# Between two blocked factorisations: T turned and B = T u^T in place of A and A u

## The reference

```
q, k, v = projections of layernorm(x)                 # 128 features each
s_t = k . q;   u = k / (|k| + eps)
Au = A u;   denom = 1 + u . Au
A  = A - Au Au^T / denom                              # A starts as the identity
M  = M + v (s_t Au / denom)^T;   o = M q
```

## Time and profile before

| what | value |
|---|---|
| median of 3 runs | 1076.78 us (1076.72 to 1078.22) |
| profiled execution, its own time | 1076.09 us |
| its span, first to last instruction | 1074.4 us |
| PE busy | 927.1 us (86%), 11675 matmul instructions and as many weight loads |
| DVE busy | 787.6 us (73%) |
| ACT busy | 543.4 us (51%) |
| mean granted TensorE clock | 0.928 of full speed |

### The profile page before, as it was taken

How to read it: one execution, slowest core, us unless ns; L and a number is a source line. 1 busy time by engine, 2 the same in 40 slices (tenths; PEclk the granted TensorE clock), 3 DMA queues, 4 the chain that set the end, 5 groups by cost and what they waited for, 6 DMA issues and landing times.

```text
span 1074.4 us, 28516 instructions
## 1 busy us (share of the span) xinstructions
PE 927.1 (86%) x11675; PEld 715.0 (67%) x11675; DVE 787.6 (73%) x2503; ACT 543.4 (51%) x1096; POOL 301.3 (28%) x256
## 2 busy tenths in 40 slices
PE   3799999999998778587996828665899999999998
PEld 1467777777785657476894627464677777777766
DVE  6878787878679998896579779793666666665663
ACT  4678787878745344222244312100366565565574
POOL 4354444444311000000000000002756446446340
PEclk9999999999999798689999868786999999999999
DMA  5343548465437462145351000266425324334131
GB/s 153 75 106 111 139 127 202 133 135 132 119 127 223 134 164 52 30 130 129 109 159 49 5 3 4 76 153 172 100 78 109 99 70 111 97 83 115 40 79 59
DMA packets 179334, 112.47 MB, mean 105 GB/s; under 512 B 79616, under 2 KB 172160, under 8 KB 178560
## 3 DMA queue, kind: packets, MB, share of 16 engines
q1 hardware_dynamic: 162304, 93.81, 34.7%
q10 hardware_dynamic: 16896, 16.78, 5.1%
HBM read 49.16 MB, written 37.75 MB: 81 GB/s over the span
## 4 chain that ended last, share of the span: by engine, by line
PE 33%; DVE 15%; issue 1%; DMA 1%; POOL 1%; ACT 1%; SPq 0%; DVEq 0%; ACTq 0%; POOLq 0%
PE ldl_work L2044 10%; PE ldl_work L2032 10%; DVE lane_rows L1156 6%; DVE ldl_rank_one L1153 4%; PE ldl_work L2016 2%; PE ldl_work L1611 2%; DVE ldl_lane_dinv L1138 2%; PE ldl_work L1621 1%; PE ldl_work L1999 1%; PE ldl_work L2007 1%; PE ldl_work L2000 1%; PE ldl_work L1986 1%; DVE lane_rows L1134 1%; DVE lane_rows L1132 1%; PE ldl_work L1428 1%
## 5 line engine op out<-in xcount | busy, mean ns | idle before, releaser
L1797 POOL TENSOR_TENSOR T<-T,out_bv_rows 128x512 f32<-128x512 f32 x16 | 20.4, 1273 | 410.4 <-DMA out_bv_rows<-in_bqkv 404.2
L446 DVE TENSOR_TENSOR ffn_h_rest<-ffn_ps_h,ffn_h_high 128x512 f16<-128x512 f32 x128 | 86.2, 685 | 56.1 <-ACT ffn_ps_h L619 55.6
L618 ACT ACTIVATE ffn_h_high<-ffn_ps_h,b_columns 128x512 f16<-128x512 f32 x128 | 87.9, 687 | 64.6 <-PE ffn_ps_h L697 64.1
L2044 PE MATMUL ldl_work<-w_ternary,ldl_panels 128*128 128x256 f16 x512 | 118.2, 273 | 0.0
L711 PE MATMUL ffn_ps_y<-w_ternary,ffn_h_high 128*128 128x256 f16 x512 | 117.8, 273 | 0.0
L711 PE MATMUL ffn_ps_y<-w_ternary,ffn_h_rest 128*128 128x256 f16 x512 | 117.8, 272 | 0.0
L697 PE MATMUL ffn_ps_h<-ffn_xT_high,w_ternary 128*128 128x512 f16 x256 | 98.7, 386 | 11.8 <-DVE ffn_h_rest L446 11.8
L697 PE MATMUL ffn_ps_h<-ffn_xT_rest,w_ternary 128*128 128x512 f16 x256 | 98.3, 384 | 0.0
L2032 PE MATMUL ldl_work<-out_xT_high,w_ternary 128*128 128x512 f16 x256 | 97.0, 379 | 0.0
L2032 PE MATMUL ldl_work<-out_xT_rest,w_ternary 128*128 128x512 f16 x256 | 97.0, 379 | 0.0
L1945 ACT ACTIVATE ldl_work<-ldl_work,b_columns 128x512 f32<-128x512 f32 x128 | 84.2, 658 | 0.0
(11 more groups left out here) (215 smaller groups left out, 2296.4 us busy)
## 6 DMA issues: line engine op xcount, KB each, us to landing
ffn_x<-in_x SPq DMA_DIRECT2D x16, 512.0 KB, 4.7
x_scratch<-ffn_x_out ACTq DMA_DIRECT2D x16, 512.0 KB, 3.3
aT_scratch<-ffn_aT SPq DMA_DIRECT2D x16, 512.0 KB, 5.2
inv_aT<-aT_scratch SPq DMA_DIRECT2D x16, 512.0 KB, 5.1
ldl_panels<-uT_scratch SPq DMA_DIRECT2D x32, 256.0 KB, 3.1
T<-x_scratch SPq DMA_DIRECT2D x16, 512.0 KB, 3.8
uT_scratch<-ffn_uT SPq DMA_DIRECT2D x16, 256.0 KB, 5.3
inv_uT<-uT_scratch SPq DMA_DIRECT2D x16, 256.0 KB, 4.2
```

Of the source, the lines that this page charges most:

```text
L446: nc.vector.tensor_tensor(hl[n % 2][:, f], ps_h[f % 3][:], hh[n % 2][:, f], ALU.subtract).then_inc(hl_done, 1)
L618: nc.scalar.activation(hh[n % 2][:, f], ps_h[f % 3][:], ACT.Gelu, bias=c.b1[:, f:f + 1])
L2044: ins = nc.tensor.matmul(ps_y[t % 2], part[k % 2][:, f, t * P:(t + 1) * P], c.w2[:, f], start=(f == 0 and part is hh), stop=(f == FC - 1 a ...
```

## The change

The stage between the factorisations no longer makes A and A u^T. With B = T u^T, the Gram matrix is B^T D^-1 B, and the right side of the second factorisation is (D^-1 B)^T T. So:

- First phase: PE turns T (transposes with the identity as moving operand), ACT copies it into `m.W`, PE multiplies it with the first 32 columns of u^T only, DVE copies these columns of B into `m.KK` and writes them times D^-1 into `first_over_d` (a view of `ZR`). The first diagonal blocks come from these two.
- Second phase: PE makes the other 96 columns of B, ACT copies them into `m.KK`; then ACT multiplies the 96 columns of each pair with D^-1 into `m.W`, 64 instructions, in front of its first `empty`.
- In the second factorisation `inject` is replaced by `multiply`: 64 matmuls per block, one for each pair, with 128 x 32 weights (columns of D^-1 B) and a moving operand of B (panel, diagonal) or T (panel right). `diagonal(r)` waits until all of D^-1 B is there.
- T must now live until panel right 3, so the finished right sides 0 to 2 get a buffer of their own, `done_right`; `keep_d(0)` waits until ACT has read the old diagonal. Six buffers of the output stage move into `done_right`.

```
@@ factorise
+        done_right = sb("done_right", [P, NW - 1, NQ, P])
+        YR = [done_right[:, k] for k in range(NW - 1)] + [m.T[:, NQ * (NW - 1):]]
...
+            if not first and r == 0:
+                sp.wait_ge(e.products.over_d, NP)
...
+        def multiply(work, r, right, dst, alone):
+            i, seen = None, set()
+            for p, q in tile_order():
+                n = NQ * q + p
+                left = e.products.first_over_d[:, n] if r == 0 else m.W[:, n, block_of(r)]
+                start = (p // 4, q) not in seen
+                seen.add((p // 4, q))
+                i = nc.tensor.matmul(work[rows_of(q), p, dst], left, right(n), start=start, stop=alone,
+                                     skip_group_check=True)
+            return i
...
-                i = inject(work, r, m.W, every, every, r == 0)
+                i = multiply(work, r, lambda n: m.T[:, n], every, r == 0)
...
-                    i = inject(work, r, m.KK, after(r), after(r), r == 0)
+                    if first:
+                        i = inject(work, r, m.KK, after(r), after(r), r == 0)
+                    else:
+                        i = multiply(work, r, lambda n: m.KK[:, n, after(r)], after(r), r == 0)
...
-            i = inject(work, r, m.KK, block_of(r), slice(0, W), r == 0)
-            if not first:
+            if first:
+                i = inject(work, r, m.KK, block_of(r), slice(0, W), r == 0)
+            else:
+                pe.wait_ge(e.products.over_d, NP)
+                multiply(work, r, lambda n: m.KK[:, n, block_of(r)], slice(0, W), False)
                 inject_units(turn_number[r, "diagonal"] % 2, r, False)
@@ gram
-                    sp.wait_ge(W_diag, before + 1)
+                    sp.wait_ge(b_done, before + 1)
...
+    def vector(v):
+        for n in range(NG):
+            v.wait_ge(b_done, n + 1)
+            nc.vector.tensor_copy(m.KK[:, pairs(n), 0:W], ps_b[n % 2][:, :, 0:W])
+            nc.vector.tensor_tensor(first_over_d[:, pairs(n)], ps_b[n % 2][:, :, 0:W],
+                                    m.dinv[:, pairs(n)].unsqueeze(2).to_broadcast([P, GROUP, W]),
+                                    ALU.mult).then_inc(B_done, 1)
+
+    def scalar(act):
+        for n in range(NG):
+            act.wait_ge(t_done, n + 1)
+            nc.scalar.activation(m.W[:, pairs(n)], ps_t[n % 2], ACT.Copy).then_inc(Tt_done, 1)
+        for n in range(NG):
+            act.wait_ge(g_done, n + 1)
+            nc.scalar.activation(m.KK[:, pairs(n), rest], ps_t[n % 2][:, :, rest], ACT.Copy).then_inc(kk_done, 1)
+        for n in range(NP):
+            act.wait_ge(kk_done, n // GROUP + 1)
+            nc.scalar.activation(m.W[:, n, rest], m.KK[:, n, rest], ACT.Copy,
+                                 scale=m.dinv[:, n:n + 1]).then_inc(over_d, 1)
+
+    def tensor(pe):
+        def turn(n):
+            if n > 1:
+                pe.wait_ge(Tt_done, n - 1)
+            for k in range(GROUP):
+                i = nc.tensor.transpose(ps_t[n % 2][:, k], m.T[:, GROUP * n + k], c.ident[:])
+            i.then_inc(t_done, 1)
+
+        def first_columns(n):
+            pe.wait_ge(u_in[n % NU], 16 * (n // NU + 1))
+            pe.wait_ge(Tt_done, n + 1)
+            if n > 1:
+                pe.wait_ge(B_done, n - 1)
+            for k in range(GROUP):
+                i = nc.tensor.matmul(ps_b[n % 2][:, k, 0:W], m.W[:, GROUP * n + k], uT[n % NU][:, k, 0:W],
+                                     start=True, stop=True)
+            i.then_inc(b_done, 1)
...
+        turn(0)
+        turn(1)
         for n in range(NG):
             if n + 2 < NG:
+                turn(n + 2)
+            first_columns(n)
             if n:
                 first_block(n - 1)
         first_block(NG - 1)
...
     def tensor_rest(pe):
+        for n in range(NG):
             x = NG + n
             pe.wait_ge(u_in[x % NU], 16 * (x // NU + 1))
+            if n < 2:
+                pe.wait_ge(Tt_done, NG)
+            else:
                 pe.wait_ge(kk_done, n - 1)
             for k in range(GROUP):
+                i = nc.tensor.matmul(ps_t[n % 2][:, k, rest], m.W[:, GROUP * n + k], uT[x % NU][:, k, rest],
                                      start=True, stop=True)
             i.then_inc(g_done, 1)
```

More of the change, by code:

```diff
@@ L885, in factorise @@
         ZR = sb("right_side", [P, NQ, P])
-        YR = [m.T[:, NQ * k:NQ * (k + 1)] for k in range(NW)]
+        done_right = sb("done_right", [P, NW - 1, NQ, P])
+        YR = [done_right[:, k] for k in range(NW - 1)] + [m.T[:, NQ * (NW - 1):]]
     works = [psum(f"work{i}", [P, NQ, P]) for i in range(1 if first else 2)]
@@ L1512, in factorise @@
     if not first:
-        e.works, e.panels, e.Z, e.ZR, e.Tt = works, panels, Z, ZR, Tt
+        e.works, e.panels, e.Z, e.ZR, e.Tt, e.done_right = works, panels, Z, ZR, Tt, done_right
         e.inject_units = inject_units
@@ L1560, in vector @@
     def vector(v):
-        def scale(n):
-            if n > 1:
[L1563 to L1586, removed]
-            if n > 1:
[L1588 to L1603, removed]
@@ L1612, in inverse @@
                                      start=True, stop=True)
-            i.then_inc(a_done, 1)
-        def times_u(n):
-            pe.wait_ge(u_in[n % NU], 16 * (n // NU + 1))
-            pe.wait_ge(A_done, n + 1)
-            if n > 1:
-                pe.wait_ge(W_done, n - 1)
-            for k in range(GROUP):
-                i = nc.tensor.matmul(ps_w[n % 2][:, k], A[n % 2][:, k], uT[n % NU][:, k], start=True, stop=True)
-            i.then_inc(w_done, 1)
+            i.then_inc(b_done, 1)
@@ L1644, in tensor_rest @@
     def tensor_rest(pe):
-        def columns(n):
+        for n in range(NG):
             x = NG + n
             pe.wait_ge(u_in[x % NU], 16 * (x // NU + 1))
-            if n == 0:
-                pe.wait_ge(W_done, NG + 1)
-            if n > 1:
+            if n < 2:
+                pe.wait_ge(Tt_done, NG)
+            else:
                 pe.wait_ge(kk_done, n - 1)
             for k in range(GROUP):
-                i = nc.tensor.matmul(ps_g[n % 2][:, k, rest], uT[x % NU][:, k], m.T[:, GROUP * n + k, rest],
+                i = nc.tensor.matmul(ps_t[n % 2][:, k, rest], m.W[:, GROUP * n + k], uT[x % NU][:, k, rest],
                                      start=True, stop=True)
             i.then_inc(g_done, 1)
-        def turn(n):
-            if n > 1:
-                pe.wait_ge(UA_done, n - 1)
-            for k in range(GROUP):
-                i = nc.tensor.transpose(ps_u[n % 2][:, k], m.T[:, GROUP * n + k], c.ident[:])
-            i.then_inc(u_done, 1)
-        for n in range(NG):
-            columns(n)
-            turn(n)
         pe.wait_ge(kk_done, NG)
-        pe.wait_ge(UA_done, NG)
     e.first_blocks, e.all_blocks = W_diag, NG
     o = Names()
+    o.first_over_d, o.over_d = first_over_d, over_d
     o.sync, o.vector, o.scalar, o.tensor, o.tensor_rest = sync, vector, scalar, tensor, tensor_rest
@@ L1707, in outputs_feed_forward @@
     rstd = sb("rstd", [P, BT])
-    xn = sb("xn", [P, BT, D])[:]
-    xh = sb("xn_high", [P, BT, D], F16)
-    xl = sb("xn_rest", [P, BT, D], F16)
-    xTh = [sb(f"xT_high{s}", [P, BT, DC, P], F16) for s in range(2)]
-    xTl = [sb(f"xT_rest{s}", [P, BT, DC, P], F16) for s in range(2)]
+    xn = place(0, 0)
+    xh, xl = (place(1, 0)[:, 2 * s:2 * s + 2].bitcast(F16).rearrange("p a (t d) -> p (a t) d", t=2) for s in range(2))
+    xTh, xTl = ([y[:, 2 * s:2 * s + 2].bitcast(F16).rearrange("p a (t d x) -> p (a t) d x", t=2, d=DC) for s in range(2)]
+                for y in (place(1, 1), place(2, 0)))
     hh = [y[:].bitcast(F16).rearrange("p (f a) x -> p f (a x)", f=FC) for y in (e.Z, e.ZR)]
```

35 lines of the change are left out of this document (14 added, 21 removed).

## The result

The changed kernel takes 1086.12 us in the median of four executions (1083.6, 1083.83, 1088.41 and 1094.58), the kernel before 1076.75 beside it. The ratio is 1.0096, 95% interval 1.0071 to 1.0121: slower by about 1%, where 1072 was predicted. The profiled execution is the fastest of the four, 1083.6 us.

The account below looks back on a forecast made before the run. Between the factorisations PE alone was taken to set the pace, then DVE's leaves. 1076.1 - 7.8 (Part 1) + 2 (Part 2) + 1.5 (part 3) = 1071.8, with the median's distance 1072; range 1066 to 1077.5.

Parts of the forecast that it names:

- rival E: Leaf 0: ACT's scaled copies cost 0.40 us each instead of 0.265, total 1080.6 us; chance 0.13.
- the row stores: Rows stored from done_right instead of T: same transfers, under leaf 3, no cost.
- part 3: Leaf 2: more PE instructions than the queue supplies make finish_diagonal(3) start short, +1.5 us (0 to +3.3).
- Part 1: First phase, up to DVE taking diagonal block 0: less PE work, -7.8 us, that take at about 544 us.
- Part 2: Leaf 0: ACT's scalings and PE's diagonal(1) end later than the leaf's cover, +2 us (-0.9 to +8).
- The row of 27 ns: Leaf 0, diagonal(1): each 128x32 product taken at 27 ns, from a row with 128 moving columns; 3.4 us at upper clock.
- B: Both leaves keep their cover because 128x32 loads overlap (11 ns): about 1069 us; chance 0.17.
- the bound for finish_diagonal(3): Leaf 2: starting with no instruction blocks in hand, its 256 matmuls take 7.2 instead of 5.3 us at worst.
- rival F: PE's instruction queue keeps pace, so leaf 2 costs nothing and leaf 0 its 2 us: 1070.3 us; chance 0.08.
- Output stage: Keeps its instructions, only its buffers lie elsewhere: no cost.

Follow-up runs that it names:

- all columns, rows, defer: Changed kernel with all 128 columns of B made in the first phase, early row stores, and panel right 2's reduce behind finish_diagonal(3): 1071.87 us, ratio 0.9946.
- scale between: Changed kernel with ACT's 64 scalings put between its copies of B instead of behind them all: median 1085.77 us, ratio 1.0057.
- inject for multiply: Changed kernel with the old 16-matmul injection in place of each multiply, D^-1 B multiplication left out: four executions, 1071.75 to 1094.24 us.
- Inject split: Kernel before the change, with each injection made in 64 matmuls instead of 16: median 1087.3 us, ratio 1.0123.
- scale, rows, defer: Changed kernel with scalings between copies, early row stores, panel right 2's reduce behind finish_diagonal(3): 1070.52, 1072.84, 1089.82, 1092.45 us; ratio of the first two 0.9943.
- Rows early: Changed kernel with rows 0 to 2 stored once panel right 3's multiplication has read T, not after the panel's whole fill: 1080.91 us, ratio 1.0036.
- its control: Kernel before the change, with rows 0 to 2 stored after panel right 3's sixteen inject instructions, not its whole fill: 1078.37 us, ratio 0.9997.
- Placement alone: Kernel before the change, with only done_right and the six moved output buffers: median 1077.27 us, ratio 1.0.
- the wide variant: Changed kernel with 128 moving columns instead of 32 in the first phase's product, nothing else: median 1092.1 us, ratio 1.0119.

## Why the prediction was wrong

The kernel got slower, which the prediction had given 0.13, and not by its rival E. Two steps failed: the row stores, put at zero, measured +5.8; and part 3, put at +1.5, measured +5.0.

**Part 1 was right.** -7.8 predicted, -8.5 measured. Take 0 at 543.46 ("about 544"), first columns 0.90 for eight.

**Part 2: the size nearly right by luck, the mechanism wrong.** +2 predicted, +2.8 measured. ACT's scalings were as worked out: 17.08/64 = 0.267 us each (0.265 predicted), their end at take + 35.0, which refutes E. But a 128 x 32 product with 32 moving columns is not 27 ns: 128 take 1.73 (580.00 to the next line at 581.73), 13.5 ns each at a granted clock of 0.50. The row of 27 ns had four times the moving columns, and the time goes with them: with 128 columns and the same weights "all columns, rows, defer" takes 3.63 us for 128, 28 ns each at 1.00. The sentence "loads over all 128 rows of the array probably don't run beside each other" chose the wrong row. So diagonal(1) ended at 583.2 (581.73 and 1.45 for the unit blocks), before DVE's release at 584.30, which by the prediction meant B, no loss. The loss came because PE's instructions ran out in finish_diagonal(1) (2.36), which followed diagonal(1) without a pause in which more could be fetched: blocks of q8 start at 581.92 and 584.98, and PE is released at 584.30. In "scale between" four start from 591.04 to 601.03, and the release comes at 605.37. How many matmuls diagonal(1) has matters less: in "inject for multiply" it has 64 instead of 160, and the leaf is 49.5, with finish_diagonal(1) starting 1.4 us late and 1.39 and 0.34 of "issue" within it. That ACT's late end is the cause is shown by "scale between".

**Part 3 was mis-sized.** +1.5 (0 to +3.3) predicted, +5.0 measured. The mechanism was right. The pace was right: 3.6 us per 128 matmuls read, 3.5 measured. PE's end of diagonal(3) was right too: 679.3, take 2 + 40.6, 6.8 us later than before against 6.2 to 8.3 worked out. Wrong was the bound for finish_diagonal(3), "7.2 instead of 5.3 at worst": PE arrived out of instructions, and before the first product 2.16 us were still due, then 2.06 and 0.61 between the products, beside the waits for ACT and DVE that stay. From D^-1 turned (679.16) to take 3 (689.72) it is 10.6 instead of the 5.5 of before. The bound counted 128 products to a block and so two blocks for 256; the rows show three, the first with 64 (L1443, above), and the wait for the first of them comes on top. "Inject split" gives that loss without the rest of the change, "inject for multiply" takes it away, "defer" too. The rule of the Trainium skill that was rival F ("Runtime: NRT & Kernel Launch", "Instruction fetch mechanics": the crossing is mostly hidden) does not hold here: leaf 2 lost 5.0 us.

**The row stores, "same transfers, under leaf 3", at zero: this failed, and it is the largest error.** +5.8 measured. The prediction asked whether PE's last product is late. It is not, as predicted: PE waits 10.07 us for DVE there. But SP hangs on PE too: its stores wait for panel right 3, panel right 3 was 4.4 us late, and twelve issues take 11.3 us. Before, they ended at 727.3, and keep_d(3) was due at 730.6, so the cover was 3.3. The row that tells this, the row stores on SP ending 3.3 us before keep_d(3), is not among those the prediction rests on. Rows early and its control show it: worth 4.3 us in the one kernel and nothing in the other. The other 1.5 of the 5.8 is about what this stretch varies by in kernels whose stores are covered (11.05 before, 11.3 and 12.3 in two others).

**Output stage: zero predicted, +2.0 in the profile.** It goes with the clock: in the five kernels with 334.6 to 335.1 the granted clock stays at 0.50 for the first 13 to 14 us of the stage, in those with 332.6 to 333.0 for 8 to 9. "Placement alone" is among the latter, so the buffers didn't do it. Why it rises later in some is left open.

**The spread.** The prediction counted the clock only as a factor in diagonal(1). After a stall of 1.4 to 2.5 us within the subtraction of panel right 3 (L1384) its 322 remaining matmuls run at 0.50, 10 to 12 us more, in four profiles; why the clock stays low while PE is busy is open. That this makes the changed kernel's 1094.58 is likely, since the wide variant shows it at 1094.07 and the mean granted clocks agree (0.909 and 0.910), but that execution has no profile of its own. The 1088.41 has 0.920, no lower than the 0.918 of 1083.6, and stays unexplained. The first phase at 0.50, seen in three other kernels, costs 20 us and would lift the changed kernel to 1103; none of its four was there.

The sum: 1083.6 = 1076.1 - 8.5 + 2.8 + 0.4 + 5.0 + 5.8 + 2.0. Of the 11.8 us between this and the 1071.8 predicted for such an execution, 3.5 are part 3, 5.8 the stores, 2.0 the output, 0.8 and 0.4 leaves 0 and 1, and -0.7 part 1.

## What to carry to other kernels

Where a stage is short of instructions, count them like work: in these rows every block of 256 PE instructions, at most 128 matmuls, took some 3.5 us, and what is left over is paid at the first point where the engine has to be on time. Look also for code that leaves part of a block unused. Ask of each late panel who waits for it on other queues: here a run of DMA issues behind it (11.3 us) was longer than its cover. Move wide, uncritical work behind the critical small products rather than ahead of them (5 us here).

## What was not expected of the hardware

- 128 x 32 weights with 32 moving columns: 13.5 ns per f32 matmul at a granted clock of 0.50 (128 in 1.73 us at 580.00), 10.8 ns at 1.00 (128 in 1.38 us, from 669.83 to the next line at 671.21). The Trainium skill, "TensorE: Matmul & The Clock Gate", section "Wait — 56ns, not 53.3ns?", states that start-to-start never drops below about 25 ns; these rows, and 64 products of 32 x 32 in 1.13 us, are below it. One product and the next write different quarters of the output rows here.
- PE's granted clock was 0.50 over long stretches in which it was busy throughout or nearly so: 51 us from the first phase on, with 32 moving columns (517.4 to 568.6 in "scale, rows, defer"), 31 to 34 us over panel right 3. With 128 columns the first phase was at 1.00 in all five profiles that have them, with 32 in two of five. Whether the added columns do it is not shown.
- Wider moving operands were nearly free with 128 x 128 weights: 1.06 us for eight instructions with 128 columns, 0.98 with 32.
- Twelve DMA issues of 256 KB in a row took SP 11.3 us, 0.58 to 1.28 each.
